# Convolution's split x and the buffers behind it moved up by 320 bytes, the masks by phase moved to the end of the scratch region

## The reference

```python
x = lax.conv_general_dilated(inputs, conv_w, window_strides=(1,), padding='SAME', ...) + conv_b
q, k, v = jnp.split(x, 3, axis=-1)          # 256 channels each
qh, kh, vh = (einsum('btd,dhe->bthe', ..) + bias)   # in blocks of 128 positions
p = softmax(where(causal, einsum('bqhe,bkhe->bhqk', qh / 8, kh), -1e9))
o = (einsum('bqhe,hed->bqd', p @ vh, wo) + bo) @ proj_w + proj_b
x = layernorm(x + o);  x = layernorm(x + ffn(x))    # ffn: base layer + 8 experts of rank 16
```

## Time and profile before

| | |
|---|---|
| three timed runs | median 1575.49 us (1565.59 to 1577.99) |
| the profiled execution | 1562.27 us; its span, from first to last instruction, 1560.5 us |
| TensorE (PE) | 1532.8 us busy, 98% |
| VectorE (DVE) | 1181.8 us busy, 76% |
| ScalarE (ACT) | 610.6 us busy, 39% |
| GpSimd (POOL) | 255.9 us busy, 16% |
| convolution | 8.65 to about 403.4 us |
| attention | to about 970 us |
| feed-forward | to the end |

### The profile page before, as it was taken

How to read it: one execution, slowest core, us unless ns; L and a number is a source line. 1 busy time by engine, 2 the same in 40 slices (tenths; PEclk the granted TensorE clock), 3 DMA queues, 4 the chain that set the end, 5 groups by cost and what they waited for, 6 DMA issues and landing times. The chain is left out here.

```text
span 1560.5 us, 29280 instructions
## 1 busy us (share of the span) xinstructions
PE 1532.8 (98%) x10816; PEld 1367.2 (88%) x10816; DVE 1181.8 (76%) x2792; ACT 610.6 (39%) x1732; POOL 255.9 (16%) x227
## 2 busy tenths in 40 slices
PE   7999999999999999999999998999999999999997
PEld 7999999999878888888888886889889989889987
DVE  8879878878876666666666677787888877878874
ACT  4324324322576767666676767211111111111110
POOL 0000000000000101000010114433333333333331
PEclk9999999999999999999999999999999999999999
DMA  8988765688610110101010213222111122111110
GB/s 324 371 309 298 281 226 201 209 299 302 235 68 8 49 54 0 54 0 54 0 54 25 85 61 95 91 75 78 60 60 60 60 74 75 63 60 60 60 58 41
DMA packets 55301, 181.05 MB, mean 116 GB/s; under 512 B 5568, under 2 KB 13888, under 8 KB 48704
## 3 DMA queue, kind: packets, MB, share of 16 engines
q1 hardware_dynamic: 53504, 173.81, 31.5%
q10 hardware_dynamic: 1728, 6.29, 1.0%
HBM read 125.49 MB, written 54.53 MB: 115 GB/s over the span
## 5 line engine op out<-in xcount | busy, mean ns | idle before, releaser
L976 ACT ACTIVATE scores_and_probs<-scores_and_probs,score_neg_max 128x128 f32<-128x128 f32 x512 | 198.1, 391 | 2.4 <-DVE score_neg_max L1077 2.4
L943 POOL TENSOR_TENSOR weights<-conv_tile,weights 128x1024 fp32r<-128x1024 f32 x14 | 35.7, 2547 | 849.5 <-ACT weights L962 764.4
L1072 DVE CUSTOM_DVE_ANT_0 scores_and_probs<-bankb,causal_mask 128x128 f32<-128x128 f32 x256 | 59.2, 288 | 114.4 <-PE bankc L1201 114.0
L1428 ACT ACTIVATE gate_exp<-h_and_gate,gate_neg_max 128x8 f32<-128x8 f32 x32 | 9.7, 302 | 347.9 <-DVE gate_neg_max L1503 347.9
L380 ACT ACTIVATE x_split<-x_planes 128x1024 fp32r<-128x1024 f32 x47 | 49.9, 1062 | 171.4 <-PE bankf L657 115.2
L1168 PE MATMUL bankg<-weights 128*128 128x512 f32 x378 | 103.2, 408 | 1.1 <-DVE v_heads L1062 1.0
L1187 PE MATMUL bankh<-weights 128*128 128x512 f32 x384 | 99.0, 393 | 1.7 <-DVE probs_T L1090 1.7
L1187 PE MATMUL banka<-weights 128*128 128x512 f32 x384 | 98.3, 391 | 0.8
L976 ACT ACTIVATION_READ_ACCUMULATOR scores_and_probs<-scores_and_probs,score_neg_max 128x1 f32 x512 | 97.4, 190 | 0.0
L1187 PEld LDWEIGHTS bankh<-weights 128*128 128x128 f32 x384 | 71.5, 188 | 19.8 <-DVE probs_T L1090 3.2
L1187 PEld LDWEIGHTS banka<-weights 128*128 128x128 f32 x384 | 71.5, 188 | 18.6 <-POOL weights L943 3.4
(11 more groups left out here) (244 smaller groups left out, 3875.0 us busy)
## 6 DMA issues: line engine op xcount, KB each, us to landing
x_raw<-in_xT SPq DMA_DIRECT2D x31, 1028.0 KB, 7.5
conv_tile<-in_x SPq DMA_DIRECT2D x32, 512.0 KB, 3.6
out<-out_tile SPq DMA_DIRECT2D x32, 512.0 KB, 2.7
conv_tile<-convT_scratch SPq DMA_DIRECT2D x16, 768.0 KB, 6.6
ce_scratch<-conv_l SPq DMA_DIRECT2D x16, 512.0 KB, 7.5
x_planes<-ce_scratch SPq DMA_DIRECT2D x16, 512.0 KB, 5.5
conv_y<-in_conv_w SPq DMA_DIRECT2D x6, 1152.0 KB, 7.5
convT_scratch<-conv_y SPq DMA_DIRECT2D x12, 512.0 KB, 7.1
```

Source lines behind the costliest of these rows:

```text
L943: nc.gpsimd.tensor_tensor(cs[:, LO, a:b, :], craw[:, a:b, :], cs[:, HI, a:b, :].bitcast(F32), ALU.subtract).then_inc(c_lo, 1)
L976: last = nc.scalar.activation(probs[:, s % 2, i, :], probs[:, s % 2, i, :], ACT.Exp, bias=ntop[:, s % 2, i:i + 1], scale=SCORE_SCALE, accu ...
L1072: last = nc.vector.tensor_tensor_reduce(out=probs[:, s % 2, i, :], in0=ps_s[h][:, n * P:(n + 1) * P], in1=mask[:], scale=1.0, scalar=LOWES ...
```

## The change

Nothing but byte offsets in the scratch region: `x_split`, `conv_m`, `conv_l`, `conv_y` and `x_raw` each move up by 320 bytes, which leaves 320 bytes unused behind `x_planes`; since `x_raw` then ends at 79232, `mask_by_phase` moves from 78912 to 81440 and ends at 83488, inside the region. `x_planes`, the weights and all buffers of the other stages stay. The order, shapes and waits of all instructions are the same on all five engines.

```diff
-    xraws = attn.at("x_raw", [P, 2, XR], F32, 62464)
-    ybuf = attn.at("conv_y", [P, TAPS * KTAPS], F32, 53248)
+    xraws = attn.at("x_raw", [P, 2, XR], F32, 62784)
+    ybuf = attn.at("conv_y", [P, TAPS * KTAPS], F32, 53568)
     wraw = [a.rearrange("p (k n) -> p k n", k=TAPS)
             for a in (craw[:, 0:TAPS * KTAPS], attn.stages[:, 0:TAPS * KTAPS], ybuf[:])]
-    lbuf = attn.at("conv_l", [P, 2 * QUAD * UQ], F32, 45056)
-    xs = attn.at("x_split", [P, XS, 2, 2, CPG, UQ], F32R, 12288)
-    mbuf = attn.at("conv_m", [P, 2, 2 * 2 * UQ], F32, 36864)
-    mask4 = attn.at("mask_by_phase", [MASK_ROWS, QUAD, P], F32, 78912)
+    lbuf = attn.at("conv_l", [P, 2 * QUAD * UQ], F32, 45376)
+    xs = attn.at("x_split", [P, XS, 2, 2, CPG, UQ], F32R, 12608)
+    mbuf = attn.at("conv_m", [P, 2, 2 * 2 * UQ], F32, 37184)
+    mask4 = attn.at("mask_by_phase", [MASK_ROWS, QUAD, P], F32, 81440)
```

## The result

| | before | after |
|---|---|---|
| median of 9 runs each, taken in turn | 1575.71 us | 1584.62 us |
| lowest to highest | 1564.47 to 1578.39 us | 1583.69 to 1585.55 us |
| the profiled execution | 1562.27 us, span 1560.5 | 1584.62 us, span 1582.8 |
| matmuls in 100 to 200 us | 885 | 836 |
| spacing of convolution's matmuls | 113.3 ns | 120.0 ns |

The ratio after to before is 1.008, with a 95% interval of 1.005 to 1.0111: the change makes the kernel slower, by about 9 us in the median. The kernel before has two levels, and without them the numbers here can't be understood. Of its 83 executions over the whole study 28 lay at 1563 to 1569 us and 53 at 1575 to 1579, with none between, and two at 2542 us, at a granted clock of 0.56, are left out here. The profiled execution of before is on the low level. The changed kernel has one level only, in these nine runs.

The account below looks back on a forecast made before the run. TensorE's matmul stream was taken to bound the kernel, busy 1532.8 of 1560.5 us. All terms summed to 0 us on the profiled 1562.27 us; the forecast was the timed median, 1575 us, range 1556 to 1592.

Parts of the forecast that it names:

- term 1: Convolution's 3456 matmuls, their moving operand x_split moved by 320 bytes: 0 ns taken, bounds -23 to +24 us.
- the faster rival: Convolution's 16 extra cycles per matmul depend on changed address bits; half to all gained: 1564 to 1552 us, chance 0.22.
- The slower rival: Convolution's weight loads and moving stream hinder each other: 5 to 7 ns per matmul, 1592 to 1599 us, chance 0.15.
- The base of the sum: Whole kernel: profiled execution's 1562.27 us, 13 us below the timed median; runs differ by 0.8%, so the median was forecast.
- All of that runs at the same 113.3 ns: Convolution's slices, at starts stepped by 1024 (weights 512) bytes, share one spacing, so such distance changes make no difference.
- Terms 2 to 4: VectorE and ScalarE on moved buffers, DMAs of x_raw, conv_y, conv_l and conv_m, and the masks: no effect taken.
- term 2: VectorE and ScalarE on moved buffers: 0 taken; 14 to 21 us idle per 100 us of convolution would hide slowing.
- The signs named: Convolution's 100 us windows: 900 matmuls or more, faster; below 865 with longer L657, slower; more TensorE idle, late operand.

Follow-up runs that it names:

- others_moved: The whole change except x_split, which stays at 12288, against the kernel before: 1576.08 us in the median, ratio 1.0013.
- all_by_64: Kernel before with x_split and everything behind it moved by 64 bytes in place of 320: 1584.7 us, ratio 1.0074.
- all_by_96: Kernel before with x_split and everything behind it moved by 96 bytes: 1573.9 us, ratio 1.0017.
- all_by_128: Kernel before with x_split and everything behind it moved by 128 bytes: 1577.58 us, ratio 1.0019.
- rows_0_too: Kernel before with heads_out and y_split at distance 0, and feed-forward weight rows padded to 1216 floats for distance 0: 1568.62 us, ratio 0.9939.

## Why the prediction was wrong

**The step that failed is term 1 of the sum**, TensorE's moving operand, taken at 0 ns per matmul. It measured +6.7 ns against the level of the profiled execution and +2.2 ns against the other. The working had all its rows right, and drew one inference that they don't bear: heads_out has the remainder by 1024 that x_split has before the change and was "slow where x_split is fast", so the low bits of the start were acquitted. Two things were wrong in it. It asked for the start of one operand, where the distance to the other one counts; x_split's and heads_out's distances are the same, 192. And it compared streams of different lengths: 233 ns at 512 columns and 113.3 at 256 are what one and the same distance gives. The row that should have raised doubt was in the text: x_split "would come to have the same remainder by 512 as the weights", the case of L1187. It was counted for the faster rival. At 512 columns it is fast, at 256 it is the worst of those measured, 120.0 ns.

**The bounds of term 1 held**: -23 to +24 us. 22.3 us between the profiled executions lie just inside. That the upper bound held is luck: its 7 ns were those of L1236 at distance 192 over L1187 at 0, both of 512 columns, where the slower distance is the one that x_split was leaving. The slower rival described what happened: a new distance between the weight load and the moving stream, 5 to 7 ns per matmul, 17 to 24 us. That the two hinder each other, as it says, is not shown beyond that dependence. Its chance of 0.15 was too low, for the inference above. Its time of 1592 to 1599 us was too high all the same, because it was laid on the median.

**The base of the sum was mis-read.** The prediction saw the profiled execution 13 us under the median and called it a spread of 0.8%. It is two levels of the very stream that the change touches, 15.8 us apart in the two profiled executions. (The middles of the two groups of times, 1565.5 and 1577.0 us, are 11.5 apart; why most low runs lie above the profiled one is open.) The rival's 22 us belong on the low level, 1562.3 + 22.3 = 1584.6, the median measured. Against the high level, where most timed runs are, it is 7.6 us by the spacing and 8.9 in the medians, about half of the least that the rival said. The three times of before (1575.49, 1577.99, 1565.59) already had the gap. This also bears on "All of that runs at the same 113.3 ns": true of that execution only.

**The faster rival** would have needed fewer than the 16 extra cycles per matmul. No kernel here came below 113.3 ns; the change doubled the extra to 32.

**Terms 2 to 4 were right.** L511 takes 1222 ns, x_raw lands after 7.2 us, and others_moved, which has all of these edits, stays at 885 matmuls per 100 us and a ratio of 1.0013. (The 14 to 21 us of idle time that term 2 gives to both engines are VectorE's; ScalarE has 65 to 71.) The stages behind convolution are only shifted: 22.1 of the 22.3 us are there when L1168 first runs.

**The signs named were the right ones.** A count under 865 and a longer L657 were to speak for the slower rival: 836, and 285 ns. No operand was late: TensorE's idle time before L657 is 8.8 us, 9.0 before.

On the two operands the Trainium skill, "TensorE: Matmul & The Clock Gate", section "Step-by-step: what each phase is for", says that TensorE has two independent read ports and that loading the next weights "doesn't steal SBUF read bandwidth from the running matmul". No run here shows the ports. But if the two did not touch each other at all, the spacing could not depend on the distance between them; it does, by up to 6.7 ns of 113.3. At distance 0 the load lasts 192 ns; at 113.3 and at 117.8 ns alike it lasts 188. The measurement decides.

## What to carry to other kernels

Where matmuls follow each other without a gap, each with a new weight load, the place of the moving operand relative to the weights is a parameter to be measured, 32 bytes at a time over 256, for each number of columns by itself. It costs no instruction, and here it was worth 6.7 ns of 113.3 in one direction and 6 of 233 in the other. When repeated times of a kernel fall into two groups, take a profile in each before anything is added to a median: the change may be worth something else on each.

## What the runs showed of the hardware

Spacing of matmuls (128x128 weights, fp32r, granted clock 1.00) by the distance of their operands:

| distance by 256 bytes | 256 columns, ns | kernels |
|---|---|---|
| 0 | 120.0 | after, all_by_64, granules moved by 64 and 320 |
| 32 | 116.7; 116.8 or 117.8 by turns | all_by_96; granule moved by 96 |
| 64 | 117.8 | all_by_128, granules moved by 128 and 384 |
| 96 | 119.9 | granule moved by 160 |
| 128 | 118.6 | granule moved by 192 |
| 192 | 113.3 or 117.8 | before, others_moved, granules moved by 0 and 256 |
| 224 | 118.3 | granule moved by 32 |

The values at 96, 128 and 224 come from one granule among others, in one kernel each.

At 512 columns distance 0 gives 226.7 ns and distance 192 gives 233. 226.7 is twice 113.3, 17 cycles of 2.4 GHz for every 16 columns. In the feed-forward rows of rows_0_too a stream of distance 0 begins at 224 to 236 ns and stays at 226 to 227 after some nine matmuls, which is why the mean of 18 is 228.9.

What was shown: at 256 columns the dependence on the distance and its period of 256 bytes; that 0 is slower than 192 at 256 columns and faster at 512; and that at distance 192 one program has two levels, chosen when the stream starts and kept, at one distance, until it is interrupted. What was not shown: what in the chip does it, what holds at 266 and 384 columns, where distance 0 gained 2 ns and nothing, why the value at distance 64 and the slower one at 192 are the same 117.8, and what chooses the level.
